# Keeping x and h in SBUF, unsplit fp32 attention, and expert lists as a table of row ids

## The reference

```
h   = layernorm(x) * (1 + ca) + sa
q, k, v = split(h @ w_qkv)                 # 16 heads of 64
q = softmax(q * SCALE, over the 64 features);  k = softmax(k, over the 4096 tokens)
context = q^T k per head;  attn = (v by context) @ w_out + b_out
x   = x + ga * attn
h   = layernorm(x) * (1 + cb) + sb
gate_probs = softmax(h @ Wg + bg)          # 8 experts, the best 2 are kept, renormalized
x   = x + gb * sum over the 2 experts of weight * (gelu(h @ W1[e] + b1[e]) @ W2[e] + b2[e])
```

## Time and profile before

| | us |
|---|---|
| median of 3 runs | 984.61 (984.42 to 986.05) |
| the profiled execution | 985.29 |
| its span, first to last instruction | 983.5 |
| TensorE busy | 834.4 (85%) |
| DVE busy | 571.4 (58%) |
| ACT busy | 453.1 (46%) |
| GpSimd busy | 277.7 (28%) |

### The profile page before, as it was taken

One profiled execution on the slowest core, in us unless ns is written; L12 is line 12 of the kernel. 1 busy time (PEld: TensorE's weight loads), 2 busy tenths in 40 slices (PEclk: granted clock), 3 DMA queues, 4 the chain that ended last, 5 costly groups with the idle time before them and its releaser, 6 DMA issues.

```text
span 983.5 us, 17834 instructions
## 1 busy us (share of the span) xinstructions
PE 834.4 (85%) x5866; PEld 769.2 (78%) x5867; DVE 571.4 (58%) x1365; ACT 453.1 (46%) x876; POOL 277.7 (28%) x206
## 2 busy tenths in 40 slices
PE   5758899999999877895019999999999999999995
PEld 4556777877877755785008999999998999989995
DVE  4777666576576535867305565465656564565553
ACT  4342554554543420111007565666657565565552
POOL 1231322312312003057741222232223222232222
PEclk9979899999999987965559999999999999999998
DMA  8501101101100075734451424333242423422222
GB/s 289 210 0 44 43 1 43 44 1 44 44 1 1 1 277 181 271 132 142 173 189 33 129 45 111 61 89 83 43 129 42 130 43 81 91 44 43 43 44 32
DMA packets 51260, 84.77 MB, mean 86 GB/s; under 512 B 4498, under 2 KB 35668, under 8 KB 51092
## 3 DMA queue, kind: packets, MB, share of 16 engines
q1 hardware_dynamic: 37396, 65.62, 19.6%
q0 software_dynamic: 13824, 18.65, 10.6%
HBM read 50.86 MB, written 33.40 MB: 86 GB/s over the span
## 4 chain that ended last, share of the span: by engine, by line
PE 63%; DVE 17%; issue 8%; POOL 5%; DMA 3%; ACT 1%; SPq 0%; DVEq 0%; ACTq 0%; POOLq 0%
PE ps L1305 20%; PE ps L1293 16%; PE ps L1100 7%; PE ps L1134 5%; POOL lists L531 4%; PE ps L1153 4%; DVE q_max L770 4%; PE ps L1210 3%; DVE k_blk L827 2%; PE ps L1276 2%; DVE w_lo L1043 2%; DMA listed<-lists 2%; DMA wmod_sb<-in_L_wmod 1%; PE ps L1204 1%; DVE ctx_acc L835 1%
## 5 line engine op out<-in xcount | busy, mean ns | idle before, releaser
L551 POOL DMA_INDIRECT out<-y,y_id x74 | 122.3, 1652 | 349.3 <-DVE y L1032 334.8
L1305 PE MATMUL ps<-w_hi,hid_hi 128*128 128x256 f32 x592 | 171.5, 290 | 12.4 <-DVE hid_lo L1023 12.4
L703 ACT ACTIVATE hid<-ps,b_col 128x256 f32<-128x256 f32 x296 | 122.2, 464 | 113.0 <-PE ps L1293 113.0
L1293 PE MATMUL ps<-xT_hi,w_hi 128*128 128x256 f32 x592 | 167.7, 283 | 2.3 <-DVE xT_lo L1004 2.3
L1023 DVE TENSOR_TENSOR hid_lo<-hid,hid_hi 128x512 fp32r<-128x512 f32 x148 | 100.6, 691 | 116.8 <-ACT hid_hi L711 115.4
L1293 PE MATMUL ps<-xT_lo,w_hi 128*128 128x256 f32 x592 | 167.4, 283 | 0.0
L1293 PE MATMUL ps<-xT_hi,w_lo 128*128 128x256 f32 x592 | 167.4, 283 | 0.0
L1305 PE MATMUL ps<-w_hi,hid_lo 128*128 128x256 f32 x592 | 166.2, 281 | 0.0
L1305 PE MATMUL ps<-w_lo,hid_hi 128*128 128x256 f32 x592 | 166.1, 281 | 0.0
L1305 PEld LDWEIGHTS ps<-w_hi,hid_hi 128*128 128x128 f32 x592 | 112.2, 190 | 16.0 <-DVE hid_lo L1023 15.6
L506 POOL TENSOR_TENSOR q_n<-q_exp,q_rec 128x1024 f32<-128x1024 f32 x32 | 60.9, 1905 | 203.7 <-DVE q_rec L778 203.7
(11 more groups left out here) (190 smaller groups left out, 1462.0 us busy)
## 6 DMA issues: line engine op xcount, KB each, us to landing
w_raw<-in_L_ffn_W SPq DMA_DIRECT2D x16, 1024.0 KB, 8.7
listed<-lists SPq DMA_DIRECT2D x38, 265.0 KB, 3.0
h_store<-h_q SPq DMA_DIRECT2D x8, 1024.0 KB, 4.0
h_b<-h_store SPq DMA_DIRECT2D x16, 512.0 KB, 6.3
x_all<-in_L_attn_x SPq DMA_DIRECT2D x8, 512.0 KB, 11.1
x_b<-in_L_attn_x SPq DMA_DIRECT2D x4, 1024.0 KB, 10.5
out<-x SPq DMA_DIRECT2D x8, 512.0 KB, 3.3
lists<-pad SPq DMA_DIRECT2D x8, 265.0 KB, 2.4
```

What stands on the lines that cost most here:

```text
L551: pool.indirect_dma_start(out[:, :], bass.IndirectOffsetOnAxis(ap=y_id[:, i:i + 1], axis=0), y[:, i, :], None, compute_op=ALU.add).then_in ...
L703: ins = act.activation(hid[:, m, :], ps[:, k, (m % 2) * BT:(m % 2 + 1) * BT], ACT.Gelu_apprx_tanh, bias=b1_col[:, bass.ds(e, 1), m])
L1293: last = pe.matmul(ps[:, k, (m % 2) * BT:(m % 2 + 1) * BT], w, a, start=st, stop=sp_)
L1305: last = pe.matmul(ps[:, Y0 + i, 0:D], a, w, start=m == 0 and st, stop=m == M - 1 and sp_)
```

## The change

- x and the transposed h stay in SBUF for the whole of stages A and B (`x_all`, `h_all`). The stores and loads of h and the second load of x are gone. SBUF is shared out anew: `b2_bc` lies where stage B's buffers lay and is loaded after them.
- The fold and h are used as plain fp32, not split: four matmuls of 256 columns for a pair of tiles. The bias is added to x by GpSimd during stage A.
- Stage B has two groups of 16 tiles. TensorE transposes x1 before normalization; the mean is taken out through the gate matrix (its column mean is subtracted) and the deviation is multiplied into the logits. ACT normalizes the rows in place, after x1 has been stored to `out`.
- Instead of lists of rows in HBM there is a table of row ids in SBUF: a place p of a list is split in p // 128 and p % 128, each as a one-hot vector, and TensorE's products of these put (token id - 4096) at its place, accumulated over all tiles in one PSUM bank.
- The normalized rows are written once in token order (`xrows`), the weights beside them. In stage C GpSimd copies 2x128 ids out of the table and gathers the rows with two indirect loads; the same ids serve the scatter. SP only loads weights there. An expert has at least two blocks.

```diff
-GT = 8
+GT = 16
-RB = 3
+CH = 4
+CHUNKS = TILES // CH
+GCH = GT // CH
+MINB = 2
...
 (SP, stage B and C)
-            def load_group(g):
...
-                sp.dma_start(listed[:, :, :], lists[bass.ds(e * CAP + b * BT, BT), :].rearrange("(p i) c -> p i c", i=BI)).then_inc(s_rows, 16)
+            load_weights(0)
...
+            for c in range(GCH + 1):
+                store_x1(c)
+            for c in range(GCH + 1, CHUNKS):
+                store_rows(c - GCH - 1)
+                store_x1(c)
+            store_rows(GCH - 1)
+            store_weights(0)
...
+            sp.wait_ge(s_wlo, 1)
+            load_weights(1)
+            sp.wait_ge(s_idxr, 1)
             sp.dma_start(b2_bc[:, :, :].rearrange("p e d -> p (e d)"), b2.rearrange("e d -> (e d)").partition_broadcast(P)).then_inc(s_b2, 16)
...
 (GpSimd)
+            def add_bias(s):
...
+                pool.tensor_tensor(x_all[:, t, :], x_all[:, t, :], bc(bo_bc[:, :], 1, [P, ST, D]), ALU.add).then_inc(s_bo, 1)
...
+            def gather(col, n):
+                pool.wait_ge(s_meta, n + ONE)
+                pool.wait_ge(s_bt, n + ONE)
+                pool.sem_inc(s_turn_pool, 1)
+                pool.tensor_copy(gid[:, :], ids[:, bass.ds(col, BI)]).then_inc(s_gid, 1)
+                pool.wait_ge(s_gid, n + 1)
+                pool.sem_inc(s_turn_pool, 1)
+                for i in range(BI):
+                    pool.indirect_dma_start(listed[:, i, :], None, xrows[:, :],
+                                            bass.IndirectOffsetOnAxis(ap=gid[:, i:i + 1], axis=0)).then_inc(s_rows, 16)
+            def scatter(col, gv):
+                pool.wait_ge(s_added, gv * 32 + DMA2)
+                pool.sem_inc(s_turn_pool, 1)
+                pool.tensor_copy(y_id[:, :], ids[:, bass.ds(col, BI)]).then_inc(s_yid, 1)
+                pool.wait_ge(s_yid, gv + 1)
+                for i in range(BI):
+                    pool.wait_ge(s_y, gv * 2 + (i + 1 + TWO))
...
             def expert(e, par, nb, last):
+                with pool.Fori(1, nb) as b:
+                    gv = now(pool, g)
+                    gather(e * COLS + b * BI, gv + 1)
+                    scatter(e * COLS + b * BI - BI, gv)
+                    pool.reg_add(g, g, 1)
+                gv = now(pool, g)
+                gather(0 if last else (e + 1) * COLS, gv + 1)
+                scatter(e * COLS + nb * BI - BI, gv)
...
 (ACT, stage B)
+            for q in range(PAIRS):
+                copy_T(q)
+                if q == 2:
+                    act.wait_ge(s_wraw, 32)
+                    for n in range(4):
+                        w_part(0, n)
+                if q >= PAIRS // 2 + 1 and q % 2:
+                    normal((q - PAIRS // 2 - 1) // 2)
+            soft(0)
+            for c in range(GCH, CHUNKS):
+                normal(c)
+            lo_hot(0)
+            lo_hot(1)
+            soft(1)
+            for c in range(2, CHUNKS):
+                if c not in LO_ON_DVE:
+                    lo_hot(c)
...
 (DVE)
-            link(dve.tensor_copy(fold_hi[:, :, :], fold[:, :, :]))
-            dve.tensor_tensor(fold_lo[:, :, :], fold[:, :, :], fold_hi[:, :, :].bitcast(F32), ALU.subtract).then_inc(s_foldr, 1)
+            dve.tensor_tensor(fold[:, :, :], ps[:, 4:6, 0:D], bc(gates[:, 0, :], 1, [P, C, D]), ALU.mult).then_inc(s_foldr, 1)
...
+            def hi_hot(c):
+                g, cc = divmod(c, GCH)
+                after(dve, s_idx, c - GCH + 1)
+                for k in range(2):
+                    for i in range(CH):
+                        last = dve.tensor_scalar(at_hi[:, cc, k, i, :], iota_hi[:, :], spot_hi[:, g, k, cc * CH + i:cc * CH + i + 1],
+                                                 token_of[:, c * CH + i:c * CH + i + 1], ALU.is_equal, ALU.mult)
...
+            dve.wait_ge(s_idx, CHUNKS)
+            link(dve.scalar_tensor_tensor(pad_t[:, :], ps[:, IX, 0:E * COLS], 0.0, pad_row[:, :], ALU.is_ge, ALU.mult))
+            dve.scalar_tensor_tensor(ids[:, :], ps[:, IX, 0:E * COLS], float(N), pad_t[:, :], ALU.add, ALU.add).then_inc(s_idxr, 1)
             dve.wait_ge(s_b2, 16)
...
 (TensorE, stage B)
+            for q in range(AHEAD):          # AHEAD = 3
+                attend(q)
+            for q in range(PAIRS):
+                rows_T(q)
+                if q + AHEAD < PAIRS:
+                    attend(q + AHEAD)
+                logits(q)
+            for g in range(GROUPS):
+                ranks(g)
+                for c in range(g * GCH, (g + 1) * GCH):
+                    index(c)
```

More of the change, by code:

```diff
@@ L447, in _ @@
[L447 to L456, removed]
-                sp.dma_start(listed[:, :, :], lists[bass.ds(e * CAP + b * BT, BT), :].rearrange("(p i) c -> p i c", i=BI)).then_inc(s_rows, 16)
[L458 to L463, removed]
-                if not isinstance(e, int):
-                    wait_reg(s_wlo, e + 2)
-                    sp.dma_start(w1_raw[:, :, :], W1[bass.ds(e + 2, 1), :, :].rearrange("a (c p) n -> p (a c) n", p=P)).then_inc(s_wraw, 16)
-                    sp.dma_start(w2_raw[:, :, :], W2[bass.ds(e + 2, 1), :, :].rearrange("a (m p) n -> p (a m) n", p=P)).then_inc(s_wraw, 16)
@@ new lines, in deviation @@
+            def deviation(g):
+                r = slice(g * GT, (g + 1) * GT)
+                dve.wait_ge(s_x1, (g + 1) * GT)
+                link(stats((g + 1) * GT // 2 - 1))
+                for t in range(r.start, r.stop):
+                    last = dve.bn_aggr(bn_a[:, t, :], bn_s[:, t, :])
+                link(last)
+                link(dve.tensor_scalar(bn_v[:, r], bn_a[:, r, 1], EPS, None, ALU.add))
+                inverse_root(bn_r[:, r], bn_v[:, r], bn_i[:, r], bn_t[:, r])
+                dve.scalar_tensor_tensor(bn_b[:, r], bn_a[:, r, 0], -1.0, bn_r[:, r], ALU.mult, ALU.mult).then_inc(s_ln2, 1)
@@ L1166, in _ @@
                     q_mm(s + 1, j // 2)
-                if s == SBN - 1 and j in (2, 3):
-                    half = j - 2
+                if s == SBN - 1 and j in (5, 6):
+                    half = j - 5
                     if half == 0:
@@ L1213, in rows_T, with attend @@
-            def rows_T(g, n):
-                t = g * GT + 2 * n
-                pe.wait_ge(s_row, t + 2)
-                pe.wait_ge(s_rTc, t // 2 - 1 + TWO)
+            def attend(q):
+                after(pe, s_x1, 2 * q - 4)
+                for i in range(2):
+                    t = 2 * q + i
+                    for c in range(C):
+                        last = pe.matmul(ps[:, AT + q % 3, i * D:(i + 1) * D], h_all[:, c, t * P:(t + 1) * P], fold[:, c, :],
+                                         start=c == 0, stop=c == C - 1)
+                last.then_inc(s_at, 1)
@@ L1265, in _, with index @@
-            ranks(GROUPS - 1)
+            def index(c):
+                cc = c % GCH
+                pe.wait_ge(s_hiA, c + 1)
+                on_dve = [b for b in LO_ON_DVE if b <= c]
+                if c in LO_ON_DVE:
+                    pe.wait_ge(s_loD, len(on_dve))
+                else:
+                    pe.wait_ge(s_loA, c + 1 - len(on_dve))
+                for k in range(2):
+                    for i in range(CH):
+                        last = pe.matmul(ps[:, IX, 0:E * COLS], at_lo[:, cc, k, i, :], at_hi[:, cc, k, i, :],
+                                         start=c == 0 and k == 0 and i == 0, stop=c == CHUNKS - 1 and k == 1 and i == CH - 1)
+                last.then_inc(s_idx, 1)
```

536 lines of the change are left out of this document (249 added, 287 removed).

## The result

| | median us | runs | ratio to before (95% interval) |
|---|---|---|---|
| before | 984.5 | 978.8 to 986.1 | |
| after | 1082.9 | 1078.4 to 1096.0 | 1.098 (1.092 to 1.105) |

The change makes the kernel 10% slower; forecast were 1005 and a range of 960 to 1055. The profiled execution of after is the slowest of its four runs (1095.95 us at a mean granted clock of 0.908, the others 1078.4 to 1086.5 at 0.914 to 0.921) and the only one with a trace, so terms read from it sum to 1096 and not to 1083, and its term for the clock is probably larger than that of the others.

The account below looks back on a forecast made before the run. The prediction took the middle as bound by DVE's routing, then GpSimd's stores, and the experts by TensorE. From 985.3 us, 31.8 saved before the experts and 51.5 added in them gave 1005, range 960 to 1055.

Parts of the forecast that it names:

- its loop: Experts: transposes, y, scatter, gather, transposes set each steady block's period, 13.36 us instead of 11.96.
- the term for the experts: Experts: late gathers add 40.6 us in 29 steady intervals and 10.9 in seven behind weight preparations, 51.5 together.
- Stage A and fold: Start of kernel: added GpSimd work hidden, fold split gone, first attention matmul at 368.6 us.
- Routing: Middle, after attention: first route ends at 430.3 us, second stops for its ranks at 447.4, table ready at 472.0.
- half clock in the middle: Rival, attention pairs: at half clock, 6.4 us rather than 3.2 each, table some 43 us later, total 1048; chance 0.09.
- First gather: Between table and experts: second gather issued at 474.0 us, first expert matmul at 483 (477 to 490), 31.8 saved.
- Experts, steady: Experts, 29 intervals without weight preparation: each gather 1.4 us late, 40.6 us added.
- The clock: Rival, experts: stalls before transposes halve TensorE's clock, 1.6 us per block, 58 us more, total 1063; chance 0.13.
- The hold: Experts: `hid_lo` on DVE could delay GpSimd's gathers 0.7 us per block, 20 us more; left out of the sum.
- The landing: Experts: gathered rows land 2.6 us after issue, taken from the trace's indirect store.
- Experts behind a preparation: Experts, seven intervals behind a weight preparation: 1.6 us more each, 10.9 us added.
- The rival that gathers land in time: Rival, experts: shorter issue, release and landing leave at most 0.8 us lag; without lag, total 953.5; chance 0.27.

Follow-up runs that it names:

- The last experiment: Kernel with the gather issued ahead of the scatter, plus the second group's ranks moved ahead of index(2) in TensorE's stream: 936.9 us, 0.950 of before.
- The first experiment: Changed kernel with the gather for block n+1 issued ahead of the scatter of block n-1 on GpSimd, gate columns copied aside: 942.7 us, 0.956 of before.
- The filler: Changed kernel with 16 extra matmuls, results unused, in TensorE's stream just ahead of the block transposes: 1071.5 us.

## Why the prediction was wrong

Its direction and its loop were right; the loop's length was not. 985.3 - 39.0 (first expert matmul) + 147.8 (36 intervals) + 1.9 (17.5 instead of 15.6 us behind the last mark) = 1096.0, the profiled execution. Forecast were -31.8 and +51.5.

The step that failed is the term for the experts, 51.5 where 147.8 was measured. Three things that the sum put at nothing make some 66 of the 96 us in between: the clock lost behind the pauses (31), the weights that now stand ahead of the gather (18), and the hold beside `hid_lo` (17). The links of the loop themselves were too short by 19 in the steady blocks, and the rest, 11, lies in the seven intervals with a preparation. In the median execution, 13 us shorter than the profiled one, the clock's part is probably smaller. It would not have been enough to put the clock alone right: the profiled execution less its 31 us is 1065, still above the range.

- **Stage A and fold**: attention at 366.8, forecast 368.6, one `fold` wait of 0.79 in place of 7.5. Right.
- **Routing**: forecast 421.6 for the deviation and 430.3 for the end of route 0; they ended 4.6 and 4.8 earlier, at 417.0 and 425.5. The steps of one route were right (8.5 us for my 8.7), the pairs were faster: 3.0 each, at a clock of 0.95 (0.70 was the mean of that whole stage before), so the rival "half clock in the middle" fell for the pairs. The stretch behind them did run at 0.50, but TensorE is busy for only 19.8 of its 54.3 us. The second route stopped for the ranks behind `index(3)`, forecast from 447.4 to 453, measured from 442.1 to 447.58. The last experiment shows that this wait was in the path.
- **First gather**: second issue forecast 474.0, measured 469.45, the 4.6 that came from the pairs; and the `b2` load, for which I added 1.2, landed in 4.7 instead of 9.4 us, ahead of the rows, and held nobody. The 1.5 us of casts that I had put behind it fell away with it. These make the 7.2 us more saved than forecast. The first expert matmul, 475.8, lies 1.2 outside my bounds of 477 to 490.
- **Experts, steady**: 29 x 13.36 = 387.4 was forecast, 454.9 measured. The 67.5 are three: the links themselves, 14.02 instead of 13.36 (0.6 more from the copy to the gather, 0.25 less for the copy, 0.3 for issues and landing), 19; the holds by `hid_lo` 17; the clock 31.
- **The clock**, the largest of the terms put at nothing. I had the mechanism and its price (1.6 per block) as a rival with a chance of 0.13, and set against it that the experts ran at 0.99. But that clock was read where TensorE was never idle for long, and my own forecast put a pause of 1.4 us ahead of every block's transposes. The pauses became 2 to 3 us, 5.6 to 6.0 at the end of six of the seven intervals with a preparation, and 20 of 29 steady blocks lost 1.5 us. The filler shows the cause. The rival itself was right in kind and not in size: it took 58 us, from all 36 blocks, and had none of the other terms. Clock and loop seem to feed each other: in the block shown y comes later, the ids meet `hid_lo`, and the next pause is 3.04 us instead of 1.99.
- **The hold** was worked out in the prediction by the Trainium skill, "SBUF — State Buffer", Who interferes with whom, at 0.7 per block and 20 us, and left out of the sum with the remark that ids and issues fall only partly beside `hid_lo`. Measured: 0.55 for the copy and 0.45 for a gather in 17 blocks, 17 us. The rule should have been in the sum.
- **The landing**: a median of 2.9 us, forecast 2.6. The fixed 2.0 us plus bytes of the Trainium skill, "DMA: Bandwidth & Descriptors", Anatomy of one DMA, gave an estimated 2.3 and would have taken the sum 11 us further off; the trace decides against it here.
- **Experts behind a preparation**: forecast 15.2, measured 19.35 in the mean of seven, 29 us together, of which 17.7 is the landing (against the 1.86 of the steady blocks). I counted SP's row load as gone and not what it had done there: SP issued the weights only behind the expert's row loads. With those loads gone, the weights start as soon as `w_lo` is done, and now stand ahead of the gather.
- **The rival that gathers land in time** fell in this order of the queue. The first experiment makes it true by another order: 985.3 - 39.0 = 946.3, measured 942.7.

## What to carry to other kernels

When a load moves to the engine that also issues the stores of results, walk round the loop before costing the load: if the load stands behind a store that waits for the work which the load feeds, the sum of all links is the period, and one static slot (the load ahead of the store, its small dependence copied aside) takes it off. A forecast stall must be put back into the clock: do not take the busy kernel's granted clock for the kernel that will have the pauses. And a queue that loses a step lets the steps behind it start earlier; ask whom they will then hold up.

## What the runs showed of the hardware

- In after a pause of TensorE of 2 us ahead of the transposes was followed by 3 us at 0.50 in some blocks and not in others (1.99 us at both 536.23 and 598.81), and the length of the pause alone does not sort them: the block at 615.41 kept 1.00 behind 3.04 us, those at 630.42 and 780.50 lost 1.6 us behind 1.70 and 1.68. With the ids copied early, pauses of 1.5 to 2.0 us cost nothing in the 22 steady blocks that don't directly follow an interval with a preparation.
- A gather of GpSimd that waits for GpSimd's own copy of the ids started 0.85 us behind it (0.90 for the first), where the second of two gathers or scatters follows by 0.30.
- An indirect load of 128 rows took 1.0 us of GpSimd and 2.9 us to landing, an indirect accumulating store 1.6 and 3.8.
- 2 MB of plain transfers (of SP) ahead of two gathers (of GpSimd) delayed their rows by some 3 us, from 2.8 to 5.7 behind the second issue, though the two lie in different queues; without the weights the delay was gone.
